# Loading two weight matrices ahead of the first column blocks, on one DMA queue of a fused transformer block

## The chip, the cores and the metric

The kernel runs on one core of one Trainium2 chip. The metric is the device time of one execution in microseconds (us), the median of several executions of the same program. An engine name in the profile stands for: PE the matrix engine (TensorE), PEld its weight loads, DVE VectorE, ACT ScalarE, POOL GpSimd, SP SyncE, which in this kernel only issues DMAs. A "q" behind an engine's name (SPq) is its instruction queue.

## The reference

The input x has the shape (4, 4096, 512), 32 MB in float32. Cut to what matters:

```python
xn  = layernorm(x)
out = x + attn(xn) + ffn(xn)

# ffn: a per-channel small MLP between two projections
s   = xn @ Win + bin_                         # 512 -> 64
h   = relu(s[..., None] * W1 + b1)            # 64 x 16
g   = einsum('btmh,mh->btm', h, W2) + b2      # -> 64
ffn = g @ Wout + bout                         # 64 -> 512

# attn: q, k, v = projections of layernorm(xn) by Wq, Wk, Wv (512 x 512);
# three rounds of attention with small 32 x 32 maps Wlq, Wlk, Wlv; the result times Wo
```

As the reference is written, its attention takes and fills only the first 16 rows of each of the 4 batches (64 rows in all); its result is added onto those rows of the output at the end. So the kernel is mostly the feed-forward part over all of x, and a small attention part woven into it.

## The kernel before, in words

**The main loop.** x is worked off in 16 tiles of 1024 rows (N = 16). A tile lies in one of six buffers `x0` to `x5` of 2 MB (named x in the profile, buffer numbers left out), half 0 and half 1 of 1 MB each. PE turns a tile (`transpose`, L466), ACT copies the turned pieces out (`evacuate`, L729), PE multiplies them by Win (`s_product`, L490), DVE and POOL make means and variances (`statistics`, L1025; `variance`, L1030 to L1035; `inv_std`, L1127), PE spreads the result (`spread_rstd`, L498; `replicate`, L520), ACT applies the 8 relus (`relu`, L755), PE sums them (`sum_h`, L536) and multiplies by Wout (`project`, L568), POOL adds the bias row onto x (`add_bias`, L1143), DVE adds the product (`add`, L998), and SP stores the tile (`store`, L265). The stages of one tile are spread over four iterations n of each engine's loop.

**Turned halves by DVE.** For tiles 0 and 1 (n < BY_PE = 2) PE turns both halves. From tile 2 on PE turns only half 0. Half 1 is loaded a second time, in a blocked layout, into three buffers `xq` (`load_quads(k)`, L250 to L256: 4 DMAs of 128 KB for each of two parts of a tile, k = 0 and 1 for tile 2, k = 2 and 3 for tile 3), and DVE turns 32 x 32 blocks with one instruction per part (`turn_quads`, L1000 to L1008, into `xqT`). `turn_quads(2, 0)` waits for the landing of part 0 and `turn_quads(2, 1)` for part 1. The result is read by `s_product(2)` on PE (L490).

**The attention's weights.** Wq, Wk, Wv and Wo (1 MB each) are loaded into halves of the still unused tile buffers: Wq and Wk into buffer 3, Wv and Wo into buffer 5 (`load_weight`, L258 and L259). PE turns them in 16 steps u of 4 transposes (L348); step u = 0, 4, 8 and 12 waits for its matrix. The turned pieces pass through two PSUM banks, which DVE (even u, L896) and ACT (odd u, L668) copy out. After step 7 PE multiplies by the turned Wq and Wk (`product_qk`, L315 to L322; the matmuls are L321), which waits for the copies of all 8 steps.

**What sets the order.** Every engine runs its instructions strictly in program order. The main loop's order is written by hand with 32 places an iteration, and the attention's steps are set among them by the lists `AT_PE`, `AT_ACT`, `AT_DVE` and `AT_POOL` (L192 to L204): a number is 32 n plus the place. On DVE, `turn_quads(2, 0)` stands ahead of the copy for step u = 6, and `turn_quads(2, 1)` follows `scale_s(1)` (L1013). On PE the copy for u = 6 is what `product_qk` waits for last.

**SP's queue.** `sp_program` (L271) issues in this order: Win, x tiles 0 and 1, bout and bo, Wq, Wk, x tile 2, then the lines that the change touches (L283 to L286), then Wout (twice), 10 small matrices and vectors and 3 scalars, x tile 3 (which waits for 8 turned steps, since it overwrites Wq and Wk), quads 2, x tile 4 (waits for `product_qk`), x tile 5 (waits for 16 turned steps), and then quads and stores in turn.

Of the kernel before, what the change touches and what calls it, by code (L numbers as in the profile page):

```python
# [20 lines left out]
def residual_block(nc, x, Wq, bq, Wk, Wv, bv, Wo, bo, lna_w, lnc_w, lnd_w, Wlq, blq, Wlk, blk, Wlv, blv,  # L21
# [35 lines left out]
    with ctx:  # L57
# [153 lines left out]
        def has(n):  # L211
            return 0 <= n < N
# [15 lines left out]
        def load(n, h):  # L228

            m = n  # L230
            if n == 3 and h == 0:
                sp.wait_ge(turned, 2 * DC)
            elif n == 4 and h == 0:
                sp.wait_ge(qk_ps, 1)
            elif n == 5 and h == 0:
                sp.wait_ge(turned, 4 * DC)
            sp.dma_start(x_sb[m][:, h * HALF:(h + 1) * HALF], x_v[n, h, :, :]).then_inc(ld[m][h], 16)
# [12 lines left out]
        def load_quads(k):  # L250

            r, n, h = k % 3, k // 2 + BY_PE, k % 2
            if k > 2:
                sp.wait_ge(tq_done, k - 2)
            for i in range(DC):
                sp.dma_start(xq[r][i * QD:(i + 1) * QD, :], xq_v[n, 2 + h, i, :, :]).then_inc(ldq[r], 16)  # L256

        def load_weight(i, w):  # L258
            sp.dma_start(w_nat[i], w.rearrange("(c p) i -> p c i", p=P)).then_inc(in_w[i], 16)  # L259

        def store(n, i):
            m = n % RING
            if n < N - 1:
                sp.wait_ge(add_done, TILES * n + 2 * (i + 1))
                sp.dma_start(out_part(n, i), by_part(x_sb[m][:, :], i)).then_inc(st[m][i], 16)  # L265
            else:
                for j in (2 * i, 2 * i + 1):
                    sp.wait_ge(add_done, TILES * n + j + 1)
                    sp.dma_start(out_v[n, :, :, j * D:(j + 1) * D], by_tile(x_sb[m][:, :], j)).then_inc(st[m][i], 16)

        def sp_program():  # L271
            sp.dma_start(win[:, :, :], Win.rearrange("(c p) m -> p c m", p=P)).then_inc(in_win, 16)
            load(0, 0)
            load(0, 1)
            load(1, 0)
            load(1, 1)
            sp.dma_start(bias_row[:, :], bout.partition_broadcast(P)).then_inc(in_rows, 16)
            sp.dma_start(row1, bo.partition_broadcast(P)).then_inc(in_rows, 16)
            load_weight(0, Wq)
            load_weight(1, Wk)  # L280
            load(2, 0)
            load(2, 1)
            load_quads(0)  # L283
            load_quads(1)
            load_weight(2, Wv)
            load_weight(3, Wo)  # L286
            sp.dma_start(wout[0:M, :], Wout).then_inc(in_wo2, 16)
            sp.dma_start(wout[M:P, :], Wout).then_inc(in_wo2, 16)
            for i, w in enumerate((Wlq, Wlk, Wlv)):
                sp.dma_start(small[:, i * HD:(i + 1) * HD], w).then_inc(in_small, 16)  # L290
            for i, v in enumerate((blq, blk, blv, lnc_w, lnd_w)):
                sp.dma_start(small[:, 3 * HD + i:3 * HD + i + 1], col(v)).then_inc(in_small, 16)
            sp.dma_start(bqc[:, :], bq.rearrange("(c p) -> p c", p=P)).then_inc(in_bq, 16)
            sp.dma_start(bvc[:, :], bv.rearrange("(c p) -> p c", p=P)).then_inc(in_bq, 16)
            for i, v in enumerate((temp, threshold, factor)):
                sp.dma_start(scal[:, i:i + 1], v.partition_broadcast(P)).then_inc(in_scal, 16)
            load(3, 0)
            load(3, 1)
            load_quads(2)
            load(4, 0)  # L300
            load(4, 1)
            load(5, 0)
            load(5, 1)
            for n in range(2, N + 3):
                if n > 2 and has(n + 1):
                    load_quads(2 * (n + 1 - BY_PE))
                if has(n - 3):
                    store(n - 3, 0)
                if has(n + 1):
                    load_quads(2 * (n + 1 - BY_PE) + 1)  # L310
                if has(n - 3):
                    store(n - 3, 1)
# [832 lines left out]
        def pool_program():  # L1145
# [90 lines left out]
            for m in range(RING):  # L1236
                for h in range(2):
                    pool.wait_ge(st[m][h], 16 * (len(range(m, N, RING)) + (1 if m == (N - 1) % RING else 0)))

        sp_program()  # L1240
        act_program()
        pe_program()
# [28 lines left out]
```

## Time and profile before

| what | us |
|---|---|
| median of 3 runs | 321.15 |
| lowest and highest | 321.01 and 324.99 |
| the profiled execution's own time | 321.15 |
| span of its profile | 319.4 |
| its mean granted clock | 0.989 |

The profile shows one execution. Its span runs from the first to the last instruction; 1.75 us of that execution's own time lie outside of it. In the timelines a row is: start, duration, engine, line, operation, what it writes and reads, its shape, how many were merged, and in brackets how long the engine sat idle before it and what ended that. "Landing" is the time from the start of a DMA's issue to its completion. A clock of 1.00 is TensorE's full clock and 0.50 the half of it.

### The profile page before, as it was taken

To read this page: it belongs to the slowest core of one execution; us is meant where nothing else is said; L and a number is where in the kernel's file an instruction comes from. 1 tells how busy PE (TensorE), PEld (TensorE's weight loads), DVE (VectorE), ACT (ScalarE), POOL (GpSimd) and SP (SyncE) were. 2 spreads that over 40 slices of the span, in tenths; PEclk is the share of its full clock that TensorE was granted. 3 is DMA by queue.
4 is the path that set the end of the run, shared out by engine and by line. 5 is a ranking of instruction groups with operands and counts; after the bars stand their busy time and mean duration, and the time that the engine had idled before them with its cause. 6 is when DMAs were issued, how large, how long until landed. Compare 5 with 4: busy or idle time off the path is not lost.

```text
span 319.4 us, 5189 instructions
## 1 busy us (share of the span) xinstructions
PE 295.4 (92%) x1819; PEld 131.8 (41%) x1819; DVE 256.4 (80%) x400; ACT 233.8 (73%) x308; POOL 237.3 (74%) x209
## 2 busy tenths in 40 slices
PE   4898899789989999999999999999999999999882
PEld 4755544335424444354443534343334343432220
DVE  0769759778699786996789999989898989895444
ACT  1548766837878869879798668888878788887940
POOL 8531999914965979479991957978969696969960
PEclk9999999979999999999999999999999999999997
DMA  7999989990669799798969999899999998323597
GB/s 237 298 372 351 325 208 344 382 272 17 197 173 350 222 334 241 250 344 231 343 179 331 294 314 303 252 364 277 329 328 363 343 354 271 148 118 153 222 279 284
DMA packets 50569, 87.80 MB, mean 275 GB/s; under 512 B 6360, under 2 KB 35184, under 8 KB 46448
## 3 DMA queue, kind: packets, MB, share of 16 engines
q1 hardware_dynamic: 46400, 65.96, 67.3%
q10 hardware_dynamic: 3504, 21.37, 18.6%
q0 software_dynamic: 640, 0.16, 0.8%
q8 instruction: 14, 0.23, 0.3%
q14 instruction: 11, 0.09, 0.1%
HBM read 53.77 MB, written 33.69 MB: 274 GB/s over the span
## 4 chain that ended last, share of the span: by engine, by line
PE 55%; DVE 26%; issue 8%; DMA 6%; POOL 4%; ACT 0%; ACTq 0%; DVEq 0%; POOLq 0%
PE op L568 13%; PE g L536 12%; PE s L490 10%; DVE stats L1025 7%; DVE x L998 6%; PE TA L466 6%; DMA out_dram<-x 3%; PE rep L520 3%; DMA b2c<-in_L_ffn_b_dram 3%; DVE xqT L1008 2%; PE op L348 2%; DVE SL L1019 1%; PE TA L321 1%; PE g L498 1%; PE TA L419 1%
## 5 line engine op out<-in xcount | busy, mean ns | idle before, releaser
L1143 POOL TENSOR_TENSOR x<-x,bias_row 128x512 f32<-128x512 f32 x128 | 163.2, 1315 | 0.0
L755 ACT ACTIVATE H<-rep,b1c,w1c 128x1024 f32<-128x1024 f32 x124 | 142.4, 1222 | 16.1 <-PE rep L520 12.2
L998 DVE TENSOR_TENSOR x<-x,op 128x1024 f32<-128x1024 f32 x59 | 71.4, 1210 | 28.1 <-PE op L568 27.7
L1025 DVE BATCH_NORM_STATS2 stats<-x 128x6 f32<-128x512 f32 x128 | 80.8, 677 | 8.3 <-DMA x<-in_L_attn_x_dram 8.3
L568 PE MATMUL op<-wout,G 64*128 64x512 f32 x236 | 65.6, 633 | 3.6 <-DVE x L998 2.8
L536 PE MATMUL g<-H,w2s 128*32 128x512 f32 x512 | 63.9, 604 | 0.0
L1127 POOL TENSOR_TENSOR rstd<-veps,nhalf 128x8 f32<-128x8 f32 x16 | 26.7, 1670 | 49.6 <-DVE veps L1035 49.6
L490 PE MATMUL s<-xT,win 128*64 128x512 f32 x128 | 58.3, 598 | 1.6 <-ACT xqT L729 1.6
L729 ACT ACTIVATE xT<-TA 128x512 f32<-128x512 f32 x64 | 38.5, 605 | 24.8 <-PE TA L466 21.8
L490 PE MATMUL s<-xqT,winq 128*64 128x512 f32 x112 | 51.1, 598 | 0.0
L466 PE MATMUL TA<-ident,x 128*128 128x128 f32 x288 | 46.7, 292 | 2.3 <-ACT xT L729 1.1
L466 PEld LDWEIGHTS TA<-ident,x 128*128 128x128 f32 x288 | 32.7, 146 | 32.6 <-issue 16.7
L1008 DVE STREAM_TRANSPOSE xqT<-xq 128x1024 f32<-128x1024 f32 x28 | 34.6, 1236 | 8.0 <-PE s L490 7.7
L490 PEld LDWEIGHTS s<-xT,win 128*64 128x64 f32 x128 | 16.2, 136 | 38.4 <-issue 38.4
L536 PEld LDWEIGHTS g<-H,w2s 128*32 128x32 f32 x512 | 12.4, 108 | 38.1 <-issue 22.6
L568 PEld LDWEIGHTS op<-wout,G 64*128 64x128 f32 x236 | 19.2, 187 | 16.4 <-issue 8.7
L520 PE MATMUL rep<-SH,spread 64*128 64x512 f32 x62 | 17.9, 574 | 0.5 <-ACT H L755 0.4
L1129 POOL TENSOR_TENSOR rwide<-rstd,ones_d 128x512 f32<-128x512 f32 x16 | 16.9, 1059 | 1.3
L1019 DVE TENSOR_TENSOR SL<-s_full,SH 128x512 fp32r<-128x512 f32 x16 | 15.8, 990 | 1.8 <-ACT SH L741 1.8
L490 PEld LDWEIGHTS s<-xqT,winq 128*64 128x64 f32 x112 | 14.2, 136 | 0.0
L762 ACT ACTIVATE G<-g,b2c 128x512 f32<-128x512 f32 x16 | 10.9, 682 | 3.5 <-PE g L536 3.5
L735 ACT ACTIVATE s_full<-g 128x512 f32<-128x512 f32 x16 | 9.5, 596 | 4.6 <-PE g L498 4.6
(176 smaller groups left out, 290.9 us busy)
## 6 DMA issues: line engine op xcount, KB each, us to landing
out_dram<-x SPq DMA_DIRECT2D x30, 1024.0 KB, 5.9
x<-in_L_attn_x_dram ACTq DMA_DIRECT2D x10, 2048.0 KB, 11.5
xq<-in_L_attn_x_dram SPq DMA_DIRECT2D x112, 128.0 KB, 7.4
x<-in_L_attn_x_dram SPq DMA_DIRECT2D x12, 1024.0 KB, 10.5
out_dram<-x SPq DMA_DIRECT2D x4, 512.0 KB, 3.3
x<-in_L_attn_Wq_dram SPq DMA_DIRECT2D x1, 1024.0 KB, 17.7
x<-in_L_attn_Wk_dram SPq DMA_DIRECT2D x1, 1024.0 KB, 19.8
x<-in_L_attn_Wv_dram SPq DMA_DIRECT2D x1, 1024.0 KB, 8.9
```

The source lines that it names most:

```text
L466: mm = pe.transpose(bank(n, g)[:, j::TILES], x_sb[m][:, col0:col0 + P], ident[:, :])
L490: mm = pe.matmul(own, w[:, c, :], turned_x, start=(c == 0), stop=(c == DC - 1))
L520: mm = pe.matmul(rep_banks(n, half)[:, b * BLK:(b + 1) * BLK], spread[own, half, :], part[own, :], start=(part is SH), stop=(part is SL), ...
L536: mm = pe.matmul(g_ps[at0:at0 + MH, :], w2s[:, half, k, :], Hr[half][k % len(Hr[half])][:, b * BLK:(b + 1) * BLK], start=(k == 0), stop=(k ...
L568: mm = pe.matmul(sum_banks(n, j)[:, b * D:(b + 1) * D], G[n % 2][own, j * P:(j + 1) * P], wout[own, :], start=True, stop=True, tile_positi ...
L729: act.activation((xT if b == 0 else xT1)[:, c, :], bank(n, g)[:, :], ACT.Copy).then_inc(ev_done, 1)
L755: act.activation(Hr[half][k % len(Hr[half])][:, :], rep_banks(n, half)[:, :], ACT.Relu, bias=b1c[:, half, k:k + 1], scale=w1c[:, half, k:k ...
L998: dve.tensor_tensor(both, both, sum_banks(n, j)[:, :].rearrange("p (h d) -> p h d", h=2), ALU.add).then_inc(add_done, 1)
L1008: dve.transpose(xqT[:, h * QH:(h + 1) * QH, :, :].rearrange("p t c a -> p (t c a)"), xq[k % 3][:, :]).then_inc(tq_done, 1)
L1025: dve.bn_stats(stats[:, j, :], x_sb[m][:, j * D:(j + 1) * D]).then_inc(bn_done, 1)
L1127: pool.tensor_tensor(rstd[:, :], veps[:, :], nhalf[:, 0:TPP], ALU.pow).then_inc(rstd_done, 1)
L1143: pool.tensor_tensor(x_sb[m][:, c], x_sb[m][:, c], bias_row[:, :], ALU.add).then_inc(xc_done, 1)
```

## The change

The loads of Wv and Wo are issued before the eight small DMAs of `load_quads(0)` and `load_quads(1)` and not behind them. Nothing else differs: the same DMAs, the same waits, the same instructions on the other engines.

```diff
@@ -280,10 +280,10 @@
             load_weight(1, Wk)
             load(2, 0)
             load(2, 1)
+            load_weight(2, Wv)
+            load_weight(3, Wo)
             load_quads(0)
             load_quads(1)
-            load_weight(2, Wv)
-            load_weight(3, Wo)
             sp.dma_start(wout[0:M, :], Wout).then_inc(in_wo2, 16)
             sp.dma_start(wout[M:P, :], Wout).then_inc(in_wo2, 16)
             for i, w in enumerate((Wlq, Wlk, Wlv)):
```

## Rows read from the trace of the kernel before

**Rows 1.** The page: busy time by engine, and the chain's shares by engine.

```profile
PE 295.4 (92%) x1819; PEld 131.8 (41%) x1819; DVE 256.4 (80%) x400; ACT 233.8 (73%) x308; POOL 237.3 (74%) x209
...
PE 55%; DVE 26%; issue 8%; DMA 6%; POOL 4%; ACT 0%; ACTq 0%; DVEq 0%; POOLq 0%
```

**Rows 2.** Chain that ended last, 0 to 120 us: start, us, what.

```profile
35.89 1.23 DVE xqT L1008
37.12 0.59 DVE x L896
37.85 3.65 PE TA L321 x16
41.51 1.02 PE op L348 x8
```

**Rows 3.** Timeline of SP's queue, 0 to 60 us.

```profile
6.03 10.88 SPq L237 DMA_DIRECT2D x<-in_L_attn_x_dram  x2
16.96 13.21 SPq L256 DMA_DIRECT2D xq<-in_L_attn_x_dram  x8
30.21 0.60 SPq L259 DMA_DIRECT2D x<-in_L_attn_Wv_dram  x1
30.85 1.88 SPq L259 DMA_DIRECT2D x<-in_L_attn_Wo_dram  x1
32.78 1.06 SPq L287 DMA_DIRECT2D wout<-in_L_ffn_Wout_dram  x1
...
41.94 2.10 SPq L237 DMA_DIRECT2D x<-in_L_attn_x_dram  x2
```

**Rows 4.** DMA issues: count, KB each, us to landing (page, then windows 6.5:16, 20.6:21.7, 28:30).

```profile
x<-in_L_attn_Wv_dram SPq DMA_DIRECT2D x1, 1024.0 KB, 8.9
x<-in_L_attn_Wo_dram SPq DMA_DIRECT2D x1, 1024.0 KB, 11.6
x<-in_L_attn_Wq_dram SPq DMA_DIRECT2D x1, 1024.0 KB, 17.7
x<-in_L_attn_x_dram SPq DMA_DIRECT2D x1, 1024.0 KB, 21.7
xq<-in_L_attn_x_dram SPq DMA_DIRECT2D x1, 128.0 KB, 13.5
xq<-in_L_attn_x_dram SPq DMA_DIRECT2D x1, 128.0 KB, 8.7
```

**Rows 5.** Timeline of the issue whose landing is 13.5, of 8.7, and of Wq's.

```profile
20.48 1.31 SPq L256 DMA_DIRECT2D xq<-in_L_attn_x_dram  x1
27.95 2.22 SPq L256 DMA_DIRECT2D xq<-in_L_attn_x_dram  x1
4.87 0.51 SPq L259 DMA_DIRECT2D x<-in_L_attn_Wq_dram  x1
```

**Rows 6.** Timeline of DVE, 0 to 75 us.

```profile
30.67 0.17 DVE L1030 TENSOR_TENSOR dmean<-stats 128x8 f32<-128x8 f32 x1
...
38.95 1.23 DVE L1008 STREAM_TRANSPOSE xqT<-xq 128x1024 f32<-128x1024 f32 x1
42.13 0.69 DVE L896 COPY WvT<-op 128x512 f32<-128x512 f32 x1 [1.95 <-PE op L348]
50.62 1.27 DVE L1030 TENSOR_TENSOR dmean<-stats 128x8 f32<-128x8 f32 x1
53.25 0.29 DVE L907 TENSOR_TENSOR centre<-ident,avg 128x128 f32<-128x128 f32 x1
61.40 3.84 DVE L925 TENSOR_TENSOR qkn<-repw,block 128x128 f32<-128x128 f32 x3
```

**Rows 7.** Timeline of PE, 0 to 76 us.

```profile
36.95 0.60 PE L498 MATMUL g<-ident,rwide 128*128 128x128 f32 x4
58.20 1.13 PE L568 MATMUL op<-wout,G 64*128 64x512 f32 x4
65.30 0.71 PE L380 MATMUL TA<-centre,qkn 128*128 128x128 f32 x4 [3.02 <-DVE qkn L925]
68.91 1.78 PE L568 MATMUL op<-wout,G 64*128 64x512 f32 x4
```

**Rows 8.** Stages: us, busy by engine (instructions), clock, DMA share, GB/s.

```profile
66.85:70.26 3.41, 3.41 (x16) 1.22 (x8) 1.87 (x3) 2.21 (x3) 0.00 (x0) 0.50 0.95 311
110.00:200.00 90.00, 88.05 (x566) 38.45 (x564) 78.98 (x123) 72.95 (x104) 67.71 (x52) 1.00 0.94 289
```

**Rows 9.** Timeline of POOL, 0 to 100 us.

```profile
34.07 17.79 POOL L1143 TENSOR_TENSOR x<-x,bias_row 128x512 f32<-128x512 f32 x14
55.11 9.98 POOL L1143 TENSOR_TENSOR x<-x,bias_row 128x512 f32<-128x512 f32 x8
```

## The prediction, made before the changed kernel ran

> **What bounds the kernel now.** I read the page first. PE is busy for 92% of the span and holds 55% of the chain of waits; DVE is second in both [rows 1]. Between 110 and 200 us PE works 88.05 of 90 us [rows 8], so whatever delays PE early on is not made up there: every instruction behind it comes later by as much. The question is therefore whether the change moves PE's work in the first 60 us. The chain of waits says how closely that stretch is knit: at 35.89 us it runs through DVE's turn of the first quads (L1008), then DVE's copy for weight step 6 (L896), then PE's product of Wq and Wk (L321), then the turning of Wv (L348), with hardly a gap [rows 2]. After that I read SP's queue and the landings, since these are all that the diff moves, and then the timelines of DVE, PE and POOL around 36 us and around 62 us.
>
> **What it gives: Wv and Wo earlier.** Wv is issued at 30.21 us and lands 8.9 us later, at 39.1; Wo is issued at 30.85 and lands at 42.4 [rows 3, 4]. PE's first use of Wv is at 41.51 us, right behind the product, with no idle time [rows 2], so Wv has been there for 2.4 us. Wo is needed after eight more groups of work, beyond 45 us; it is not late either. The gain is 0. It could be above 0 only if PE waited for one of them, and it doesn't.
>
> **What it takes: the quads later.** The fourth DMA of quads 0 is issued at 20.48 us and lands 13.5 us later, at 34.0; the last of quads 1 is issued at 27.95 and lands 8.7 us later, at 36.6 [rows 4, 5]. DVE turns them at 35.89 and 38.95 us [rows 2, 6]: 1.9 and 2.3 us of margin. The landings come one behind the other in the order of issue: the last quads 36.6, Wv 39.1, Wo 42.4. So the transfers are queued up and only their sum counts, and quads 0 will land later by what the 2 MB of Wv and Wo take. From the last quads to Wo that is 42.4 - 36.6 = 5.8 us, with some of Wout's 256 KB among it. The nearest other 2 MB are Wk and the first half of tile 2, issued behind Wq: Wq lands at 4.87 + 17.7 = 22.6 and the half tile (issued at 6.03) at 6.03 + 21.7 = 27.7, which gives 5.2 us [rows 3, 4, 5]. The slower of the two weights alone took 3.3 us, so 6.6 is the upper bound. I take 5.5. Quads 0 then land at 34.0 + 5.5 = 39.5 and quads 1 at 42.1.
>
> DVE stands in program order, so it waits from 35.89 to 39.5: **3.6 us** (bounds: 34.0 + 5.2 - 35.9 = 3.3, and 34.0 + 6.6 - 35.9 = 4.7). Queued behind the wait is the copy for step 6, and PE's product waits for that. It starts 1.96 us after the turn starts (37.85 - 35.89), so at 41.45 and not at 37.85 [rows 2]. PE has nothing else to do: its last work before is the spreading at 36.95, 0.60 long, so its queue stands from 37.55 to 41.45, 3.9 us [rows 7]. For quads 1 DVE would come at 38.95 + 3.6 = 42.55, after the landing at 42.1; and behind it DVE idles 1.95 us for PE anyway [rows 6]. Quads 1 cost 0, and would up to some 2 us of lateness.
>
> **SP's queue.** It issues the eight quads in 13.21 us because it is held up by the transfers before them; then Wv and Wo in 2.5 us [rows 3]. Together they fill 16.96 to 32.78 us in either order, Wout starts where it did, and the fifteen issues up to 41.94 are bound by their own durations. Tile 3 is issued at 41.94 as before: it waits for step 7, which comes before the stall. Tile 4 waits for the product; tile 5 for step 15, which comes some 5 us later, but it stands in line behind other transfers. I cost this at 0; half a us either way would be hidden, since no tile is used the moment it lands in this stretch.
>
> **The clock.** An idle PE has a second price. At 62.28 to 65.30 PE idled 3.02 us for DVE's L925 [rows 7], and in 66.85 to 70.26 its granted clock was 0.50, so 1.2 GHz in place of 2.4 [rows 8]. There four matmuls of L568 took 1.78 us and not 1.13 [rows 7]. In 3.41 us at half clock PE, which was busy throughout, does 1.7 us of work, so the price is **1.7 us**. The new idle time of 3.9 us is longer than the one that was followed by this, so I count the price once. Its bounds are 0 (the low clock falls into the idle time itself) and 3.4 (two such stages).
>
> **What comes back.** POOL's 14 bias adds from 34.07 to 51.86 don't wait for the quads [rows 9]. L925 is three DVE operations of 128x128 that take 3.84 us, 1.28 each, beside POOL's next eight bias adds at 55.11 to 65.09; a like one (L907), at a time when POOL did none, took 0.29 [rows 6, 9]. DVE's work at 45 to 52 us, now 5.3 us later, falls partly behind the first 14 adds, so it sheds some 1.1 us that it loses there today (L1030 took 1.27 us at 50.62 and 0.17 at 30.67, when POOL added nothing [rows 6]); POOL's next adds, which start from DVE's variance, then come only 4.2 us later and DVE's L925 5.3 us. The last of the three operations then runs free: 1.28 - 0.29 = **1.0 us** back. PE's second gap shrinks from 3.0 to 2.0 us, and may then not be followed by the low clock: half of 1.7, **0.8 us** back. The bounds are 0 and 3 x 1.0 + 1.7 = 4.7.
>
> A rule of the Trainium skill bears on this: the page SBUF — State Buffer, section "Who interferes with whom", says that a DVE instruction with two SBUF inputs and a GpSimd instruction that reads SBUF take one shared port by turns, each for its whole length. The trace agrees: 1.28 us for an operation of 0.29 is about the length of one bias add (17.79 / 14 = 1.27). By this rule the last operation comes free only if the eight adds are over when it starts, so the sum with it is the one above; without it, the 1.0 us would be gone.
>
> **The sum.** 3.6 + 1.7 - 1.0 - 0.8 = +3.5 us on the profiled execution's own 321.15, which is also the median of the runs: 324.6 us. Its own range is 3.3 + 0 - 1.8 = +1.5 to 4.7 + 1.7 - 0 = +6.4.
>
> **The rivals.**
> *The delay is given back in full (not slower).* The place is L925 with PE's gap at 62 us. If DVE's delay makes all three operations miss POOL's adds, 3.0 us come back, and the second low clock with its 1.7 us goes as well. With the shortest stall and no low clock behind the first gap that is 3.3 - 4.7 = -1.4, or 319.8 us; with one low clock +0.3, or 321.5. It decides from the point where POOL's adds end before L925 begins, 3.8 us earlier than today relative to DVE. For it: both ends are that close today, and POOL isn't held by the quads. Against it: POOL's eight adds are themselves started by DVE's variance, so most of the shift is common to both.
> *The stall is longer in its wake.* Two low stages and no give-back: 4.7 + 3.4 = +8.1, or 329.3; with the stall as forecast, 3.6 + 3.4 - 1.0 = +6.0, or 327.2. For it: half-speed PE right after a long idle. Against it: the one case in the trace lasted a single stage of 3.41 us.
> *The quads are not held up.* If the transfers of the quads ran beside those of Wv and Wo and ended within the 1.9 us of margin, nothing would move: 321.2. Against it speak the landings in order of issue. The Trainium skill (DMA: Bandwidth & Descriptors, "Queues, rings and completion order") says that each DMA engine consumes one queue's descriptors in ring order though completions may overlap; by this the overlap is small and the sum stays.
>
> **How the numbers follow.** Forecast 0.6 (324.6 us); given back in full 0.15 (319.8 to 321.5, or 320.8); longer 0.13 (327 to 329.3, or 328); not held up 0.12 (321.2). The range that leaves out no more than 2 in 10 is 320.5 to 328.0. A difference of 2%, 6.4 us, is about what a measurement of this kernel can tell from none. Slower by more than that needs 327.6: half of the third case, 0.06. Faster by that needs 314.7, which nothing gives: 0.01. The same: 0.93.
>
> **What would show it.** Right: Wv lands near 33.5 and Wo near 36.5 us; quads 0 near 39.5; DVE's L1008 shows some 3.6 us of idle time ended by the DMA of the quads, and PE's L321 starts near 41.4 with the copy L896 as its releaser; half clock for some 3.4 us soon after; L925 under 3.84 us. Wrong: L1008 at 36 us without a wait (the quads were not held up), or PE's work after 66 us at its old times although the product was late (the stall was absorbed).

## The result, and the profile after

| | before | changed |
|---|---|---|
| median of 20 runs, us | 323.35 | 324.95 |
| lowest to highest | 321.01 to 324.99 | 323.86 to 327.43 |
| span of the profiled execution | 319.4 | 324.0 |

The changed kernel takes 1.0063 times as long as the kernel before (95% interval 1.004 to 1.0086), about 2 us; the two medians of the table stand 1.6 us apart. A ratio and its interval, here and below, leave out the executions that took over 1.5% more than the fastest one of the same kernel. The 20 runs of the kernel before, made beside it, have a median of 323.35 us; the execution profiled earlier, at 321.15, lies at the lower end of them, and the changed kernel's profiled one (324.0 us of span) is slightly above its median. So the two profiles stand 4.6 us apart where the kernels stand 2 us apart: they show the mechanisms, and the intervals show the size. The median of the kernel before is 2.2 us above the 321.15 us that the forecast started from.

Timeline of SP's queue in the changed kernel, the counterpart of [rows 3]:

```profile
17.01 0.65 SPq L259 DMA_DIRECT2D x<-in_L_attn_Wv_dram  x1
17.71 2.79 SPq L259 DMA_DIRECT2D x<-in_L_attn_Wo_dram  x1
20.54 16.17 SPq L256 DMA_DIRECT2D xq<-in_L_attn_x_dram  x8
36.75 0.97 SPq L287 DMA_DIRECT2D wout<-in_L_ffn_Wout_dram  x1
...
45.07 0.91 SPq L237 DMA_DIRECT2D x<-in_L_attn_x_dram  x2
```

Wout is issued at 36.75 us and not at 32.78, tile 3 at 45.07 and not at 41.94. Further on SP stands for PE. The issue of tile 5 in the kernel before, the same in the changed kernel, and what SP waited for there between 28 and 100 us:

```profile
50.20 0.81 SPq L237 DMA_DIRECT2D x<-in_L_attn_x_dram  x2
```

```profile
56.02 0.80 SPq L237 DMA_DIRECT2D x<-in_L_attn_x_dram  x2
...
SPq L237 <- PE op L348: 3.3, 1, 3.3
```

Tile 5 waits for PE's weight step 15 (L348). PE ends it at 50.17 us in the kernel before and at 55.98 in the changed one, so tile 5, and quads 3 right behind it, are issued 5.8 us later by PE's delay; SP had been ready at 52.7 us.

The DMA of quads 0 that DVE waits for is the fourth; its row among the issues (count, KB, us to landing) is

```profile
xq<-in_L_attn_x_dram SPq DMA_DIRECT2D x1, 128.0 KB, 9.7
```

It was issued at 30.42, so it lands at 40.1. DVE's timeline of the changed kernel, beside [rows 2, 6]:

```profile
40.15 1.25 DVE L1008 STREAM_TRANSPOSE xqT<-xq 128x1024 f32<-128x1024 f32 x1 [4.08 <-DMA xq<-in_L_attn_x_dram]
41.32 0.65 DVE L896 COPY x<-op 128x512 f32<-128x512 f32 x1
...
43.08 1.23 DVE L1008 STREAM_TRANSPOSE xqT<-xq 128x1024 f32<-128x1024 f32 x1
...
51.17 0.79 DVE L1019 TENSOR_TENSOR SL<-s_full,SH 128x512 fp32r<-128x512 f32 x1 [0.51 <-ACT SH L741]
...
67.22 2.05 DVE L925 TENSOR_TENSOR qkn<-repw,block 128x128 f32<-128x128 f32 x3
...
73.04 1.25 DVE L1008 STREAM_TRANSPOSE xqT<-xq 128x1024 f32<-128x1024 f32 x1 [1.44 <-DMA xq<-in_L_attn_x_dram]
```

PE's timeline, beside [rows 2, 7]:

```profile
37.05 0.60 PE L498 MATMUL g<-ident,rwide 128*128 128x128 f32 x4
42.02 5.30 PE L321 MATMUL TA<-x,xnT 128*64 128x512 f32 x16 [4.37 <-DVE x L896]
47.25 1.09 PE L348 MATMUL op<-ident,x 128*128 128x128 f32 x8
...
69.33 0.71 PE L380 MATMUL TA<-centre,qkn 128*128 128x128 f32 x4 [1.24 <-DVE qkn L925]
```

The stages 41.96 to 45.38 and 42 to 50 us, with columns as in [rows 8]:

```profile
41.96:45.38 3.42, 3.36 (x8) 1.00 (x10) 2.35 (x4) 0.00 (x0) 3.42 (x4) 0.50 0.20 3
42.00:50.00 8.00, 7.98 (x39) 3.17 (x40) 3.03 (x5) 1.79 (x3) 8.00 (x7) 0.79 0.42 90
```

and 42 to 50 us of the kernel before:

```profile
42.00:50.00 8.00, 8.00 (x65) 3.91 (x63) 6.04 (x9) 4.03 (x7) 8.00 (x7) 1.00 0.85 275
```

How to read them together. PE's product of Wq and Wk (L321) starts 4.2 us later (42.02 for 37.85), because its last operand's copy (L896) stands behind DVE's turn of the quads, and that behind the landing. The stage at 0.50 begins as PE resumes; L321 takes 5.30 us and not 3.65. PE's next step (L348) is 5.8 us late (47.25 for 41.44). At L380 only 4.0 us of this are left (69.33 for 65.30), and the half clock that followed L380 before [rows 8] doesn't come, so that L390, some 6 us further on, is 2.7 us late (75.51 for 72.78). The last rows show something that the prediction did not have: in 42 to 50 us the DMA engines moved 90 GB/s and not 275. SP's rows say why: from 36.75 to 45.07 us it issued small transfers only, and tile 3 after them.

### The profile page after: what moved, and what is told of

Read it like the earlier page. It is cut to its first block, busy times and chain, and to the rows that moved or that the text cites. A ratio compares the mean times of both kernels' runs of the same rounds, so it can differ in the third digit from the quotient of the medians.

```text
span 324.0 us, 5189 instructions
## 1 busy us (share of the span) xinstructions
PE 295.2 (91%) x1819; PEld 131.0 (40%) x1819; DVE 253.2 (78%) x400; ACT 234.4 (72%) x308; POOL 236.2 (73%) x209
## 4 chain that ended last, share of the span: by engine, by line
PE 41%; DVE 24%; DMA 11%; SPq 10%; issue 7%; POOL 4%; ACT 2%; ACTq 0%; DVEq 0%; POOLq 0%
PE op L568 10%; PE g L536 9%; DMA xq<-in_L_attn_x_dram 7%; DVE stats L1025 7%; PE s L490 7%; DVE x L998 7%; SPq L237 4%; PE TA L466 4%; SPq L256 4%; DMA out_dram<-x 3%; PE rep L520 2%; DVE SL L1019 2%; DVE xqT L1008 2%; PE TA L321 2%; POOL x L1143 1%
## 5 line engine op out<-in xcount | busy, mean ns | idle before, releaser
L1019 DVE TENSOR_TENSOR SL<-s_full,SH 128x512 fp32r<-128x512 f32 x16 | 15.5, 971 | 1.8 <-ACT SH L741 1.8
```

## The experiments

All ratios are to the kernel before, run on the same chip beside each. They were run in three groups, on three chips: copy_first_after to psum_after in the first; psum_busy_after, psum_after_2, wv_only and between in the second; the others in the third. The kernel before has a median of 322.18 us in the first group, 323.55 in the second and 324.01 in the third, so ratios, not medians, are compared across groups. Even ratios move: one and the same kernel has 1.0105 as psum_after and 1.0052 as psum_after_2. A difference of half a per cent between groups is therefore read as none.

| kernel | ratio | 95% interval |
|---|---|---|
| the change | 1.0063 | 1.004 to 1.0086 |
| copy_first_after | 1.0046 | 1.0017 to 1.0075 |
| busy_after | 1.0139 | 1.01 to 1.0179 |
| psum_before | 0.9909 | 0.9876 to 0.9942 |
| psum_after | 1.0105 | 1.0075 to 1.0135 |
| psum_busy_after | 1.0047 | 1.001 to 1.0084 |
| psum_after_2 | 1.0052 | 1.0022 to 1.0082 |
| wv_only | 0.9993 | 0.9962 to 1.0025 |
| between | 0.9975 | 0.9935 to 1.0016 |
| between_pool | 0.9959 | 0.992 to 0.9999 |
| before_pool | 0.9908 | 0.9871 to 0.9945 |
| psum_busy_pool_after | 1.0064 | 1.0029 to 1.0099 |
| best_before | 0.9836 | 0.98 to 0.9872 |

### Is the copy behind DVE's wait what PE stands for? copy_first_after

```diff
-            -32, -32, 13, 13, 32, 34, 36, 40, 41, 41, 48, 48, 48, 64, 69, 69, 73, ...
+            -32, -32, 13, 13, 32, 34, 36, 40, 41, 41, 48, 48, 48, 48, 69, 69, 73, ...
```

> The changed kernel, with DVE's copy for weight step 6 put ahead of the turn of quads 0 (one entry of the list of places for DVE, 64, made 48). My theory: PE's 4.4 us of idle time before the product of Wq and Wk comes only from that copy queued behind DVE's wait for the late quads. Then the product starts near 37.6 us again and at full clock; DVE still waits some 3.5 us for the quads until 40.1, so its copy for step 8 comes at about 44.3 and PE loses about 1.5 us there. The time: 2 to 3.5 us under the changed kernel's minus what the shorter gap before L380 gave back, so between the kernel before and 2 us above it. Rival (the DMA queue's new order is itself the cost, wherever DVE waits): the product still starts after 41 us and the time stays at 325.

Measured 1.0046. DVE's and PE's timelines:

```profile
36.74 0.69 DVE L896 COPY x<-op 128x512 f32<-128x512 f32 x1 [0.75 <-PE op L348]
40.39 1.25 DVE L1008 STREAM_TRANSPOSE xqT<-xq 128x1024 f32<-128x1024 f32 x1 [2.96 <-DMA xq<-in_L_attn_x_dram]
...
70.85 1.25 DVE L1008 STREAM_TRANSPOSE xqT<-xq 128x1024 f32<-128x1024 f32 x1 [3.10 <-DMA xq<-in_L_attn_x_dram]
```

```profile
37.88 3.65 PE L321 MATMUL TA<-x,xnT 128*64 128x512 f32 x16 [0.30 <-issue]
...
44.59 1.09 PE L348 MATMUL op<-ident,x 128*128 128x128 f32 x8 [1.03 <-DVE WvT L896]
...
73.33 0.70 PE L390 MATMUL TA<-qT,bd 128*128 128x256 f32 x2 [1.88 <-DVE bqk L933]
```

The quads are as late as in the changed kernel, and still the product starts at 37.88 and runs at full clock; PE loses 1.03 us later instead. The place of PE's stall is shown by this. The time is 0.2% under the change's, within the two intervals: of the rival, that the queue's new order costs the same wherever DVE waits, the product's start is refuted and the time is not. The last rows say why so little was gained: DVE waits again, until 70.85 us, now 3.10 us for quads 3, and PE for DVE at L390. Here SP never waited for PE, so the lateness of quads 3 comes from the new order alone. The stage 42 to 50 us agrees, at 25 GB/s, less still than in the changed kernel:

```profile
42.00:50.00 8.00, 6.97 (x58) 3.08 (x55) 7.25 (x12) 4.17 (x7) 8.00 (x7) 1.00 0.28 25
```

### What the half clock and the give-back are worth: busy_after, psum_before, psum_after

busy_after keeps PE at work where it would idle, ahead of `product_qk`'s waits:

```diff
+            pe.wait_ge(xnT_made, 1)
+            for _ in range(34):
+                pe.transpose(A_ps[:, 0:P], ident[:, :], ident[:, :])
             pe.wait_ge(turn_dve, DC)
             pe.wait_ge(turn_act, DC)
-            pe.wait_ge(xnT_made, 1)
```

> The changed kernel, with 34 transposes of the unit matrix, which nothing reads, on PE ahead of its wait for the copy of step 6 (0.13 us each by the rows, 4.4 us in all). My theory: the clock falls to 0.50 only because PE idles; kept busy it stays at 1.00, the 16 matmuls of L321 take 3.65 us and not 5.30, and all that follows up to the gap before L380 comes 1.7 us earlier than in the changed kernel; the stall of 4.2 us stays. Time 1.7 us under the changed kernel's, if L925 still loses its wait for POOL as it does there; 0.5 to 1 us less gain if it does not. Rival (the low clock has another cause, such as a regular cut): L321 still takes over 5 us and the time is that of the changed kernel.

Half a miss. The product ran at full clock, as its row shows (this kernel's line numbers are 2 higher):

```profile
42.31 3.65 PE L323 MATMUL TA<-x,xnT 128*64 128x512 f32 x16 [0.22 <-DVE x L898]
```

But the ratio was 1.0139, above the change's. So the low clock at this place follows PE's idling, and the 1.65 us that it costs there did not come off the kernel's time. Why the time rose is open: at L390 (L392 here) its profile is 0.6 us ahead of the changed kernel's (74.95 for 75.51), but the execution profiled, 324.08 us, is the fastest of its six.

psum_before and psum_after make L925 read the replicated small weights from PSUM, in the kernel before and in the changed one:

```diff
-ins = dve.tensor_tensor(heads(nat[:, i, :]), rep[:, i * HD:(i + 1) * HD].unsqueeze(1).to_broadcast([P, hpc, HD]),
+ins = dve.tensor_tensor(heads(nat[:, i, :]), A_ps[:, i * HD:(i + 1) * HD].unsqueeze(1).to_broadcast([P, hpc, HD]),
```

> The kernel before, with the three products of L925 reading the replicated small weights from the PSUM bank and not from their copy in SBUF, so that only one input lies in SBUF. My theory: L925 took 3.84 us because each of its three operations waited for a bias add of POOL. Now the three take under 1 us together beside the same bias adds, PE's gap of 3.0 us before L380 shrinks to about 0.3, no half clock follows it (1.65 us), and the time falls by 3 + 1.65 = 4.6 us, to about 318.5 against 323.3. Rival (L925 is slow by itself): it still takes over 3 us and the time is that of the kernel before.

> The changed kernel, with the same edit of L925. In the changed kernel L925 took 2.05 us and no half clock followed, so here the edit is worth only about 1.3 us: about 323.7. My theory: the change costs 5.8 us at PE up to L380 and gets 3.3 us of it back there, since L925 ran partly free of POOL and PE's gap was too short for the clock to fall. With the edit in both kernels nothing is left to give back, so this kernel stands 5 to 6 us over psum_before, where the change alone stands about 2 us over the kernel before. Rival (the give-back is elsewhere, or the delay is absorbed by later slack): this stands no more than 2.5 us over psum_before.

Measured 0.9909 for psum_before, 1.0105 for psum_after, and 1.0052 for psum_after_2, the same kernel in the second group. psum_before's rows of DVE and PE:

```profile
62.18 0.69 DVE L925 TENSOR_TENSOR qkn<-TA,block 128x128 f32<-128x128 f32 x3
...
66.93 1.25 DVE L1008 STREAM_TRANSPOSE xqT<-xq 128x1024 f32<-128x1024 f32 x1 [1.40 <-DMA xq<-in_L_attn_x_dram]
```

```profile
62.99 0.71 PE L380 MATMUL TA<-centre,qkn 128*128 128x128 f32 x4
```

The same three products take 0.69 us, not 3.84, beside the same bias adds; PE's idle time of 3.02 us before L380 is gone, and the clock stays at full. The kernel before gains 0.9%, 2.9 us, and not the 4.6 that I expected: DVE now waits 1.40 us for quads 3, which land at 66.9 us here, so their landing stands behind L925 in the old order too. The changed kernel gains nothing from the edit (1.0105 and 1.0052 against 1.0063), where I had expected 1.3 us; DVE waits 1.88 us for quads 3 in psum_after.

With the edit in both kernels, the change costs 1.0105 / 0.9909 = 1.020 by the first group and 1.0052 / 0.9909 = 1.014 by psum_after_2, 4.6 to 6.4 us, where alone it costs 2 us. The profiles show it ahead of the wait for quads 3: L380 starts at 69.06 us in psum_after and at 62.99 in psum_before, 6.1 us apart, where it is 4.0 without the edit. So at L925 the kernel before loses what the changed kernel doesn't, and the give-back is shown. Its size end to end, 2.6 to 4.4 us by the ratios, is not that of L925 alone, since the later landing of quads 3 is in it as well.

### How far the load order matters: wv_only, between

wv_only puts Wv alone ahead of the quads; between puts both weights between quads 0 and quads 1. Both are shown against the changed kernel:

```diff
             load_weight(2, Wv)
-            load_weight(3, Wo)
             load_quads(0)
             load_quads(1)
+            load_weight(3, Wo)
```

```diff
-            load_weight(2, Wv)
-            load_weight(3, Wo)
             load_quads(0)
+            load_weight(2, Wv)
+            load_weight(3, Wo)
             load_quads(1)
```

> Only the load of Wv goes ahead of the quads; Wo stays behind them. My theory: the landing of quads 0 moves with the bytes put ahead of it: 1 MB takes 2.7 us, so quads 0 land near 37 us, DVE waits about 1.0 us (margin 1.9), PE's product starts 1.0 us later than before, its idle time of 1.4 us is too short for the clock to fall, and the time is within 1 us of the kernel before's. Rival (any larger transfer ahead of the quads costs about the same, by blocking SP's issues): a wait of 3 us or more, half clock in L321, and a time like the changed kernel's.

> Wv and Wo are put between quads 0 and quads 1. My theory: only quads 0 matter, since behind the turn of quads 1 DVE has 1.95 us of idle time. Quads 0 land at 34 us as before, no wait; quads 1 land near 42, DVE waits some 3 us for them, the product starts at its old time with full clock, and the copy for step 8 comes 1 us late, so PE loses 0.4 to 1 us there. Time within 1 us of the kernel before's. Rival (lateness of either part costs in full): 3 us at PE and a time like the changed kernel's.

wv_only came out at 0.9993, as expected, but on another path. DVE waited 1.97 us and not 1.0, and half clock followed a gap of 2.26 us on PE, shorter than the 3 us seen so far. At L390 its PE is 2.3 us later than in the profile of the kernel before (75.08 for 72.78), while the runs of the two are level: single profiles differ by that much without the kernels' times differing. The row with the gap:

```profile
39.88 5.35 PE L321 MATMUL TA<-x,xnT 128*64 128x512 f32 x16 [2.26 <-DVE x L896]
```

In between (0.9975) quads 0 landed in time, the product ran at 37.90 at full clock, DVE waited 3.26 us for quads 1, and PE lost 0.65 us of it: quads 0 matter and quads 1 nearly don't, as expected. Then came two rows that I had not foreseen, one of DVE and one of PE:

```profile
45.52 6.43 DVE L1019 TENSOR_TENSOR SL<-s_full,SH 128x512 fp32r<-128x512 f32 x1
```

```profile
53.80 1.66 PE L348 MATMUL op<-ident,x 128*128 128x128 f32 x8 [3.89 <-DVE WoT L896]
```

L1019 takes 0.69 us alone and 6.43 here. Its end, 51.95, lies half a us behind that of POOL's burst of 14 bias adds, 51.41:

```profile
34.11 17.30 POOL L1143 TENSOR_TENSOR x<-x,bias_row 128x512 f32<-128x512 f32 x14
```

### Is it POOL's burst? between_pool, before_pool

Both get one wait, ahead of POOL's tenth add of the burst; between_pool is between with it, before_pool the kernel before with it:

```diff
+                if n == 2:
+                    pool.wait_ge(sl_done, 2)
                 if has(n - 1):
                     add_bias(n - 1, 1)
```

> The kernel of between with one wait more: POOL doesn't start its tenth bias add of the burst of 14 before DVE's L1019 of tile 1 is done. In between, L1019 took 6.43 us (45.52 to 51.95) and ended with POOL's burst, and PE idled 3.89 us behind it, with half clock after. My theory: DVE's L1019, which has two inputs in SBUF, is kept off by POOL's adds as long as one follows the other. With the wait it takes under 2 us, PE's gap of 3.89 us and the half clock behind it are gone, and the profile's PE is 3.5 to 5 us earlier at the turning of Wo; the time falls by 1 to 4 us, since not every execution of between need have had the long wait. Rival (L1019 waits for something else): still over 4 us, no gain.

> The kernel before with the same wait on POOL. Its executions lie at 321 to 322 us and at 323.5 to 325. My theory: the upper ones had a longer L1019 (1.66 us in the one profiled), by the same contention; with the wait the upper group goes and the median falls by 0.5 to 2 us. Rival (the two groups come from the clock or another place): the spread and the median stay.

In between_pool L1019 took 0.68 us, at nearly the same time, and POOL paused 1.05 us for it:

```profile
45.63 0.68 DVE L1019 TENSOR_TENSOR SL<-s_full,SH 128x512 fp32r<-128x512 f32 x1
```

```profile
46.39 6.23 POOL L1143 TENSOR_TENSOR x<-x,bias_row 128x512 f32<-128x512 f32 x5 [1.05 <-DVE SL L1019]
```

PE's gap of 3.89 us is gone. The ratio is 0.9959 against between's 0.9975; by these intervals that is no difference, where I had expected 1 to 4 us. Part of the reason is in its profile: at L380 PE now idles 2.51 us for L925, and half clock follows. So the 6.43 us were the burst's doing, which is shown for the profiled execution; that all executions of between had them is not. before_pool took 0.9908, 3 us less than the kernel before and more than I expected; over all of its 12 runs the medians stand 2.6 us apart and the means 1.7, which is within what I expected. Its runs still lie between 318.72 and 324.34 us: the spread stayed, so L1019 alone doesn't make it. L1019 took 0.69 us in its profile and L925 2.87, where it had been 1.66 and 3.84, so the gain isn't that of L1019 alone.

### Is the gain of the clock handed to POOL? psum_busy_after, psum_after_2, psum_busy_pool_after

psum_busy_after joins the edits of psum_after and busy_after. psum_after_2 is psum_after again. psum_busy_pool_after adds the wait of POOL.

> The changed kernel with both edits: L925 reads from PSUM, and 34 idle transposes keep PE busy while it would wait for the copy of step 6. In busy_after the product of Wq and Wk ran at full clock (3.65 us), but the time did not fall, and its profile has a gap of 2.16 us before L380 again, where the clock may fall in other executions. Here that second gap is gone. My theory: the half clock behind the stall is worth 1.7 us, so this stands 1.2 to 2.0 us under psum_after_2 of the same call. Rival (the dummy work costs PE as much as the clock gives, or the clock falls elsewhere instead): no difference beyond 0.5 us.

> The kernel of psum_after again, beside the one above, on the same chip: it was 1.05% over the kernel before. Both theories expect that again, within 0.3%; it is the reference for psum_busy_after.

> The kernel of psum_busy_after with the same wait on POOL. There the full clock brought PE's product 1.7 us forward, but L1019 then came at 49.6 us, still within POOL's burst, took 2.90 us, and no time was gained against psum_after_2 (325.1 and 324.3). My theory: the clock's 1.7 us were handed to POOL's burst; with POOL held back the gain shows, and the time is 1 to 2.5 us under psum_after_2's ratio of 1.005, so at 0.998 to 1.002 of the kernel before. Rival (the dummy work itself costs): no gain, 1.005 as before.

The first missed: 1.0047 against 1.0052. In its profile PE is 3.3 us earlier than in psum_after_2 after the product (45.67 for 48.98; in psum_after_2 the half clock lasted 6.8 us and the product 6.57), and L1019 took 2.90 us, by which part of it went. But at L390 it was still 2.3 us ahead (73.34 for 75.64), and where that went is open. psum_after_2 missed as well: it was to come within 0.3% of psum_after's 1.0105. The last missed too: with POOL held back L1019 took 0.69 us, and the ratio was 1.0064. So my account of POOL's burst as the taker was too narrow. The edit is also less gentle here than in between_pool, since L1019 comes 4 us later: it holds POOL for 5.32 us and not for 1.05, which may cost something of its own.

```profile
50.55 6.23 POOL L1145 TENSOR_TENSOR x<-x,bias_row 128x512 f32<-128x512 f32 x5 [5.32 <-DVE SL L1021]
```

DVE's and PE's rows of psum_busy_pool_after show another taker (line numbers 2 higher again):

```profile
72.93 1.25 DVE L1010 STREAM_TRANSPOSE xqT<-xq 128x1024 f32<-128x1024 f32 x1 [3.76 <-DMA xq<-in_L_attn_x_dram]
```

```profile
75.40 0.96 PE L392 MATMUL TA<-qT,bd 128*128 128x256 f32 x2 [2.80 <-DVE bqk L935]
```

Quads 3 are turned at 72.93 us, against 73.04 in the changed kernel and 67.50 before. At L380 this kernel's PE is 3.1 us ahead of psum_after_2's (66.63 for 69.74); at L390 it is 0.2 us ahead, it has idled 2.80 us, and half clock follows. In the seven kernels profiled with both weights ahead of quads 0 the last DMA of quads 3 lands between 70.8 and 73.5 us; it was issued between 56.0 and 60.5, and the later issues were not the later landings. That landing is a floor under everything that makes PE faster ahead of it. The old order has the same floor some 5 us earlier, at 65.9 to 67.5 us.

### A faster version: best_before

The old load order with L925 from PSUM, the copy of step 6 ahead of the turn, and POOL's wait.

> The order of loads of the kernel before, with three edits: L925 reads from PSUM, DVE's copy for step 6 stands ahead of the turn of quads 0, and POOL waits as in before_pool. Expected: at least psum_before's gain (0.9909), with 0.3 us from the copy and 0.5 to 1 us from POOL's wait: 0.986 to 0.990. If the theory of POOL's burst is wrong, it stays at 0.991.

0.9836 (0.98 to 0.9872), some 5 us under the kernel before: the fastest of all, and a little more than I expected. The three edits are those already shown. It does not escape quads 3 either, as its rows of DVE and PE and the stage behind them show:

```profile
67.55 1.25 DVE L1008 STREAM_TRANSPOSE xqT<-xq 128x1024 f32<-128x1024 f32 x1 [2.94 <-DMA xq<-in_L_attn_x_dram]
```

```profile
70.03 0.70 PE L390 MATMUL TA<-qT,bd 128*128 128x256 f32 x2 [1.98 <-DVE bqk L933]
71.13:74.54 3.41, 3.41 (x15) 1.66 (x15) 3.40 (x6) 1.90 (x4) 1.15 (x1) 0.50 0.90 204
```

## Why the prediction was right, point by point

The forecast was 324.6 us from 321.15, so +3.5; the profiled pair shows +4.6 and the runs 2 us. That the median of 324.95 lies so near to 324.6 is luck: the start was 2.2 us too low and the difference 1.5 us too large.

*What it gives, 0.* Right. Wv landed at 34.1 us, 13 us before PE used it at 47.25, and no wait for a weight went away, since there had been none.

*The stall, 3.6 us.* Right in place and cause. It measured 4.2 us at PE and 4.08 us on DVE, since quads 0 landed at 40.1 and not at 39.5, within the bounds of 3.3 to 4.7. copy_first_after shows the path by the one entry that undoes it; between shows that quads 1 cost little. That the stall is what the 2 us of the kernel consist of is not shown: without it, copy_first_after costs 1.0046, which can't be told from 1.0063, as the landing of quads 3 holds it up instead.

*SP's queue, 0.* This step failed. I took it that the issues fill the same time in either order. The eight quads took 16.17 us to issue and not 13.21, Wout's issue came 4.0 us later and tile 3's 3.1 us later. With only small transfers issued meanwhile, the DMA engines moved 90 GB/s between 42 and 50 us and not 275, and the loads after that are late: the last half of tile 4 lands at 64.4 us and not at 58.2, quads 3 at 73.0 and not at 65.9. I had also put tile 5 in line behind other transfers; in both kernels it was step 15 that released it. So two causes meet in the 7.1 us of quads 3. In copy_first_after, where SP had no wait for PE, their last DMA was issued at 56.02 us and not at 58.78, and landed at 70.8: the new order alone makes 4.9 us. The rest is not separated; in the changed kernel this DMA landed 3.6 us behind the one issued just ahead of it, where it was 0.6 in the kernel before, and why is open. DVE turns the quads at 73.04 us, after a wait of 1.44 us that it did not have before. I had called half a us hidden; the lateness was 6 to 7 us, and what hid most of it was that DVE and PE were late too. This is why the total came out well with a step missing. It costs PE 0.2 us in the changed kernel, but 1.88 in copy_first_after and 2.80 in psum_busy_pool_after.

*The clock, 1.7 us.* Right as a row: L321 took 5.30 - 3.65 = 1.65 us more. As a term of the time it is not shown: three kernels that kept PE busy there gained nothing. L1019 (2.04 and 2.90 us in two of them) and the landing of quads 3 (in the third) took some of it back in the profiles; the rest is unexplained.

*What comes back, 1.8 us.* The mechanism was right, the size too small. L925 came 5.8 us later and POOL's eight adds 3.9, so the two moved against each other by 2.0 us and not by 1.1: DVE shed 1.10 us at L1030, as forecast, and 0.87 at L1019 (1.66 to 0.79), which I had left out. L925's three operations took 0.58, 1.35 and 0.28 us, so the last ran free, the first waited for the end of an add only, and 3.84 - 2.05 = 1.8 us came back and not 1.0. PE's gap shrank from 3.02 to 1.24 us and not to 2.0, and the half clock behind it stayed away in full: between L348 at 47 us and L390 5.8 - 2.7 = 3.1 us came back in the profile. This is the term that was mis-sized. With it the profile stands at +2.7 us at L390, where the forecast had 3.5; that the 2 us between the runs come from the same is likely, but no run separates it. The rival "given back in full" was the nearer one on this point. The psum pair is in line with the other side of the sum: with L925 out of it the change costs 4.6 to 6.4 us, and 3.6 + 1.7 is 5.3; but quads 3 are in those numbers too, so the sum is not confirmed by them.

The rule of the Trainium skill on the shared port (SBUF — State Buffer, "Who interferes with whom") is borne out by psum_before: with one of the two inputs in PSUM the same three operations take 0.69 us together, beside POOL's adds. What I took from it, turns with a wait of one bias add, 1.27 us, is too little: in between L1019 waited for five.

*What stays open.* Between 77 us and the end another 1.9 us comes up between the two profiles, in steps of 0.5 to 1 us at ACT's and DVE's waits; no run was made for them, and single executions of one kernel differ by more. Why the kernel before has runs at 321 and at 324 us is open as well.

## What to carry to other kernels

Before a load is moved ahead, ask for each load that falls back how long it lies landed before its use, and what stands on the consumer's engine behind that use: here 1.9 us of margin and one copy decided. A queue of loads is also a queue of issues: here two larger transfers ahead of eight small ones delayed the issue of all that followed, the DMA engines ran at a third of their rate for 8 us, and the loss appeared some 25 us later as a floor. The same queue can also wait for the very engine that the change delays, as tile 5 did. And a local gain, like the full clock over the product, gave nothing here that the runs could tell, as other waits (a port, a landing) stood behind it. Before a stall is called the cost, undo it alone and time the kernel: here the time hardly moved.

## What the runs showed of the hardware that was not expected

DVE's operation on two SBUF inputs (L1019, 0.69 us by itself) was held for 6.43 us in between, till POOL's back-to-back bias adds had ended, where in the kernel before, at 45.35 us and in the same burst, it took 1.66. It starts within 0.2 us of the same time in both, so the wait is not a matter of one add. One pause of POOL of 1.05 us removed it.

A gap of 2.26 us on PE was followed by half clock in wv_only, and so was one of 1.98 us in best_before (0.50 from 71.13 to 74.54 us), while gaps of 2.06 to 2.17 us in before_pool, copy_first_after, busy_after and wv_only (all before L380) were not. In busy_after the clock was at 0.50 from 22.95 to 26.36 us as well, behind a gap of 1.34 us. The length of the gap alone doesn't tell whether the clock falls.
